# Router scores with the tokens as stationary operand, and five stages moved in a hand-written schedule of two expert layers on one Trainium2 core

## The reference

```python
x = x + L0_xattn(_layernorm(x), ids, ctx, ctx, ctx)      # 4 experts of 256 rows, one per token
x = x + L0_ffn(_layernorm(x), Wg, W1, W2, W3)            # 8 experts of 176 rows, two per token

# layer 2
scores = jnp.einsum('btd,ed->bte', x, Wg)
topk_s, topk_i = jax.lax.top_k(scores, TOP_K)
probs = jax.nn.softmax(topk_s, axis=-1)
...
    h = jax.nn.silu(jnp.einsum('btd,hd->bth', x, W1[e])) * jnp.einsum('btd,hd->bth', x, W2[e])
    y = y + w[..., e:e + 1] * jnp.einsum('bth,dh->btd', h, W3[e])
```

## Time and profile before

| | |
|---|---|
| median of 3 runs | 169.12 us (169.01 to 169.64) |
| the profiled execution, its own time | 168.78 us |
| its span in the trace | 167.0 us |
| PE busy | 153.6 us (92%) |
| DVE busy | 111.9 us (67%) |
| ACT busy | 67.0 us (40%) |
| POOL busy | 59.7 us (36%) |
| HBM | 52 GB/s over the span |

### The profile page before, as it was taken

The page is one execution under the profiler, slowest core; times in us unless marked ns, Lnnn a source line. Parts: engine busy times, 40 slices in busy tenths (PEclk is TensorE's granted clock), DMA queues, the critical chain, the costliest instruction groups (busy, mean ns, idle before and its releaser), DMA issues.

```text
span 167.0 us, 2431 instructions
## 1 busy us (share of the span) xinstructions
PE 153.6 (92%) x892; PEld 131.2 (79%) x892; DVE 111.9 (67%) x223; ACT 67.0 (40%) x119; POOL 59.7 (36%) x49
## 2 busy tenths in 40 slices
PE   7399999959999888999999979999999999999991
PEld 2078788738998666888888868888888888888890
DVE  0858998946695957499999792964444744444453
ACT  3266864624616560835437342206222222222210
POOL 0569967829765871459527300000000000000000
PEclk9969999999999999999999999999999999999999
DMA  3975263030330012051000000000000300000003
GB/s 107 327 271 162 57 214 110 0 94 2 98 96 0 0 12 85 4 144 44 0 0 4 0 0 0 2 4 0 0 0 0 113 16 0 0 0 4 2 0 126
DMA packets 4332, 8.76 MB, mean 52 GB/s; under 512 B 736, under 2 KB 864, under 8 KB 4320
## 3 DMA queue, kind: packets, MB, share of 16 engines
q1 hardware_dynamic: 4176, 8.60, 16.2%
q10 hardware_dynamic: 144, 0.00, 0.0%
HBM read 7.55 MB, written 1.05 MB: 52 GB/s over the span
## 4 chain that ended last, share of the span: by engine, by line
PE 48%; DVE 24%; issue 10%; POOL 6%; ACT 6%; DMA 3%; SPq 1%; ACTq 0%; DVEq 0%; POOLq 0%
PE z L669 27%; PE y L694 19%; DVE act L572 6%; DVE act_lo L537 6%; POOL gated L327 4%; DMA raw<-weights_dram 3%; DVE stats L453 2%; ACT act_hi L377 2%; DVE hT_lo L477 2%; POOL w_lo L281 1%; PE y L612 1%; DVE norm L470 1%; DVE x_sb L483 1%; ACT silu L405 1%; DVE gated L562 1%
## 5 line engine op out<-in xcount | busy, mean ns | idle before, releaser
L669 PE MATMUL z<-hT_hi,w_hi 128*128 128x512 f32 x120 | 47.7, 398 | 0.3 <-ACT hT_hi L351 0.2
L669 PE MATMUL z<-hT_hi,w_lo 128*128 128x512 f32 x120 | 47.2, 393 | 0.0
L537 DVE TENSOR_TENSOR act_lo<-act,act_hi 128x512 fp32r<-128x512 f32 x38 | 33.9, 891 | 16.9 <-ACT act_hi L377 16.7
L694 PE MATMUL y<-w_hi,act_lo 128*128 128x256 f32 x152 | 43.2, 284 | 1.2 <-DVE act_lo L537 1.2
L694 PE MATMUL y<-w_hi,act_hi 128*128 128x256 f32 x152 | 43.0, 283 | 0.0
L694 PE MATMUL y<-w_lo,act_hi 128*128 128x256 f32 x152 | 43.0, 283 | 0.0
L405 ACT ACTIVATE silu<-z 128x512 f32<-128x512 f32 x38 | 22.7, 597 | 46.6 <-PE z L669 46.6
L669 PE MATMUL z<-hT_lo,w_hi 128*128 128x512 f32 x120 | 37.5, 393 | 1.9 <-DVE hT_lo L477 1.8
L281 POOL TENSOR_TENSOR w_lo<-raw,w_hi 128x768 fp32r<-128x768 f32 (+1 forms) x15 | 28.2, 1888 | 15.3 <-ACT w_hi L342 15.3
L694 PEld LDWEIGHTS y<-w_hi,act_lo 128*128 128x128 f32 x152 | 29.0, 191 | 3.3 <-DVE act_lo L537 1.8
L377 ACT CAST act_hi<-act 128x512 fp32r<-128x512 f32 x38 | 23.4, 616 | 20.1 <-DVE act L572 19.1
(11 more groups left out here) (51 smaller groups left out, 79.5 us busy)
## 6 DMA issues: line engine op xcount, KB each, us to landing
raw<-weights_dram SPq DMA_DIRECT2D x11, 384.0 KB, 3.2
raw<-weights_dram SPq DMA_DIRECT2D x8, 256.0 KB, 5.2
x_sb<-x_dram SPq DMA_DIRECT2D x4, 256.0 KB, 4.8
out_dram<-x_sb SPq DMA_DIRECT2D x4, 256.0 KB, 2.5
consts_sb<-consts_dram SPq DMA_DIRECT2D x1, 68.0 KB, 3.8
ids_sb<-token_ids_dram ACTq DMA_DIRECT2D x1, 4.0 KB, 4.0
router_raw<-router_dram SPq DMA_DIRECT2D x1, 8.0 KB, 2.8
```

The lines of the kernel that those rows point to most:

```text
L537: nc.vector.tensor_tensor(act_lo[:, i, :], act[:, i, :], act_hi[:, i, :].bitcast(F32), ALU.subtract)\
L669: return nc.tensor.matmul(bank[:], w[b][:, c, cols], tokens[:, h, k, :], **flags)
L694: last = nc.tensor.matmul(o, a[:, q % BUFFERS, rows], w[b][:, c, wd], start=(first and j == 0), stop=(c == CHUNKS[b] - 1 and j == 2), skip ...
```

## The change

Two kinds of edits. First, the router's scores: `route_scores` makes, for each of the four tiles of 128 tokens, six products that add up in 8 columns of `y[h][0]`, with the tokens (`hT_hi` or `hT_lo`, 128x128) as stationary operand and 8 columns of the router as moving operand. That is 24 products a half in place of 4 of 512 columns. The result has tokens on partitions, so the copy `score_rows`, the four `transpose_scores` and the addition of two parts in `best_two` are gone. All 24 now stand behind the wait for both `hT_lo` tiles. Second, moves: for layer 1 half 1, `normalise` goes from q = 5 to 4 and `tokens_lo` from 7 to 6 on DVE, and `tokens_hi` at q = 7 (and for layer 2 half 0, where it was so before) goes ahead of `round_act` on ACT; for layer 2 half 0, `transpose_gates` goes from q = 16 slot 1 to q = 17 slot 0, and `gates_out` from q = 15 to 16; for layer 2 half 1, `best_two` goes from q = 24 to 23. POOL makes the `_lo` part of weight piece (1, 3) behind the gating of step 15 and not ahead of it.

```diff
-    "normalise": (5, 3, 4),
+    "normalise": (4, 3, 4),
     "transpose_tokens": ((7, 0), (6, 0), (6, 1)),
     "tokens_hi": (7, 5, 6),
-    "tokens_lo": (7, 4, 5),
+    "tokens_lo": (6, 4, 5),
     "scores": (None, (7, 0), (7, 0)),
-    "score_rows": (None, 7, 7),
-    "transpose_scores": (None, (7, 1), (7, 1)),
-    "best_two": (None, 7, 8),
+    "best_two": (None, 7, 7),
     "tanh": (None, 7, 8),
     "softmax": (None, 7, 8),
-    "transpose_gates": ((3, 0), (8, 1), (10, 1)),
-    "gates_out": (2, 7, 9),
+    "transpose_gates": ((3, 0), (9, 0), (10, 1)),
+    "gates_out": (2, 8, 9),
...
+LATE_LO = (1, 3)
...
+                if LATE_LO in SPLIT_AT.get(q - 1, ()):
+                    weight_lo(*LATE_LO)
                 for piece in SPLIT_AT.get(q, ()):
-                    if piece not in VECTOR_LO:
+                    if piece not in VECTOR_LO and piece != LATE_LO:
                         weight_lo(*piece)
...
-                first_tokens = (1, 0) in due("tokens_hi", q)
-                if first_tokens:
-                    tokens_hi(1, 0)
+                first_tokens = [way for way in due("tokens_hi", q) if way != (1, 1)]
+                for way in first_tokens:
+                    tokens_hi(*way)
                 if q >= 1:
                     round_act(q - 1)
...
-                dve.wait_ge(scores_T, h + 1)
-                sc = y[h][1][:, 0:HALF_TILES * 2 * EXPERTS2].rearrange("p (t a e) -> p t a e", a=2, e=EXPERTS2)
-                link(nc.vector.tensor_copy(score_part[:], sc[:, :, 1, :]))
-                link(nc.vector.tensor_tensor(score[:], sc[:, :, 0, :], score_part[:], ALU.add))
+                dve.wait_ge(scored, h + 1)
+                link(nc.vector.tensor_copy(score[:], y[h][0][:, 0:HALF_TILES * EXPERTS2].rearrange(
+                    "p (t e) -> p t e", e=EXPERTS2)))
...
                 pe.wait_ge(hT_lo_done, KD * ln_no(1, h) + 1)
-                for k in range(KD):
-                    nc.tensor.matmul(y[h][0][0:2 * EXPERTS2, :], router_hl[:, k, :, :].rearrange("p a e -> p (a e)"),
-                                     hT_hi[:, h, k, :], start=(k == 0), stop=False, skip_group_check=True)
                 pe.wait_ge(hT_lo_done, KD * ln_no(1, h) + KD)
-                for k in range(KD):
-                    last = nc.tensor.matmul(y[h][0][0:EXPERTS2, :], router_hl[:, k, 0, :], hT_lo[:, h, k, :],
-                                            start=False, stop=(k == KD - 1), skip_group_check=True)
+                for i in range(HALF_TILES):
+                    cols = slice(i * P, (i + 1) * P)
+                    for k in range(KD):
+                        for j, (tokens, part) in enumerate(((hT_hi, 0), (hT_hi, 1), (hT_lo, 0))):
+                            last = nc.tensor.matmul(y[h][0][:, i * EXPERTS2:(i + 1) * EXPERTS2], tokens[:, h, k, cols],
+                                                    router_hl[:, k, part, :], start=(i == 0 and k == 0 and j == 0),
+                                                    stop=(k == KD - 1 and j == 2), skip_group_check=True)
                 last.then_inc(scored, 1)
-
-            def transpose_scores(h):
-
-                pe.wait_ge(score_rows_done, h + 1)
-                for i in range(HALF_TILES):
-                    last = nc.tensor.transpose(y[h][1][:, i * 2 * EXPERTS2:(i + 1) * 2 * EXPERTS2],
-                                               score_rows[:, i * P:(i + 1) * P], ident[0:2 * EXPERTS2, 0:2 * EXPERTS2])
-                last.then_inc(scores_T, 1)
```

More of the change, by code:

```diff
@@ L165, in ffn_moe @@
         minus_half = sb("minus_half", [P, TILES])
-        score_part = sb("score_part", [P, HALF_TILES, EXPERTS2])
         score = sb("score", [P, HALF_TILES, EXPERTS2])
@@ L169, in ffn_moe @@
         top_i = sb("top_i", [P, HALF_TILES, 8], U32)
-        score_rows = sb("score_rows", [2 * EXPERTS2, HALF])
         gap = sb("gap", [P, HALF_TILES])
@@ L192, in ffn_moe @@
         hT_hi_done, hT_lo_done = sem("hT_hi_done"), sem("hT_lo_done")
-        scored, score_rows_done, scores_T = sem("scored"), sem("score_rows_done"), sem("scores_T")
+        scored = sem("scored")
         gap_done, th_done = sem("gap_done"), sem("th_done")
@@ L417, in _ @@
                         tokens_hi(*way)
-                for _, hh in due("score_rows", q):
-                    act_e.wait_ge(scored, hh + 1)
-                    nc.scalar.copy(score_rows[:], y[hh][0][0:2 * EXPERTS2, :]).then_inc(score_rows_done, 1)
                 for _, hh in due("tanh", q):
@@ L718, in stages @@
                     route_scores(hh)
-                for _, hh in due("transpose_scores", q, slot):
-                    transpose_scores(hh)
             pe.wait_ge(warm_in, 1)
```

## The result

The changed kernel takes 171.6 us (170.68 to 171.85, 4 executions) against 169.2 of before: ratio 1.0128, 95% interval 1.0086 to 1.0171. It is slower, where the forecast was 1.4 us faster, and 171.6 lies above the upper end of its range, 169.4. The profiled execution took 171.64 us, span 169.8.

What follows compares the result with a forecast made beforehand. PE, busy 92% of the span, was taken to set the time. Terms of -2.1, -0.2 and +0.9 summed to -1.4 us, giving a forecast of 167.6 us against 169.12 before, range 165.3 to 169.4.

Steps and rivals of the forecast that it cites:

- the clock stays at 1.00 behind both: Expected profile sign: PE's granted clock stays at full speed behind the short score products of both layer 2 halves.
- the rival on the clock: Short score products count as idling and lower PE's clock: 169.3 us for one fall, 171.0 for two; chance 0.05 each.
- The price of 24 products: Layer 2 scores: each short product takes 0.119 us, so 2.85 us a half, bounds 1.7 and 4.6.
- The tokens of half 1: Layer 1 half 1: hT_lo starts earlier, at 32.8, shortening PE's wait in up(8): -2.1 us, bounds -2.4 to -1.3.
- Half 0, scores and gates: Layer 2 half 0: PE's wait for gate_rows goes, up(18) waits about 0.28 us and starts slightly earlier: -0.2 us.
- Half 1: Layer 2 half 1: scores wait 0.4 us for the second hT_lo, then 24 products take 2.85 us: +0.9 us.
- the sentence that I let DVE's lag behind PE stand: Layer 2, 70 to 95 us: DVE's lag behind PE was assumed unchanged, as its work hangs on the same gates.

Runs made afterwards that it cites:

- e2: The kernel before with only the new score form, 24 products of 8 columns a half, all else in its old place: median 172.31 us, ratio 1.021 to before.
- e6: e1 with normalise of layer 1 half 1 back at q = 5: median 165.52 us, ratio 0.979 to before.
- e9: The changed kernel with normalise at 5 and 16 score products a half, their 16 moving columns repeated to 128: median 165.27 us, ratio 0.983 to before.
- e12: e9 with the gates of layer 2 half 0 at their old place: median 164.67 us, ratio 0.984 to before.
- e3: The changed kernel with the router's 8 moving columns repeated to 128 in each score product: median 168.44 us, ratio 1.000 to before.
- e1: The kernel before with the moves alone, scores in their old form: median 167.01 us, ratio 0.990 to before.
- a_again: The changed kernel itself, taken again later: median 171.44 us over 10 executions, ratio 1.006 to before.
- e5: The changed kernel with the router's 8 moving columns repeated to 32 in each score product: median 170.21 us, ratio 0.999 to before.
- e14: The changed kernel with normalise at 5 and the gates at their old place: median 167.63 us, ratio 0.996 to before.
- e13: e6 with 48 extra products of 8 columns in one piece behind down(30) in layer 2, result unused: median 175.39 us.
- e11: e6 with the gates of layer 2 half 0 back at their old place: median 164.58 us, ratio 0.981 to before.

## Why the prediction was wrong

- **The step that failed** is "the clock stays at 1.00 behind both", with the rival on the clock at 0.10. The mechanism stood in that rival with its price (1.7 us a fall; measured 1.66 and 1.69), but I gave it one chance in ten and cut the range below it. The argument against it was that PE's idle 1.81 us in the earlier trace rows had not brought the clock down. That was one execution, and in e2's profile a fall follows the same wait; and the short products last longer than that wait, 2.6 us, which the argument didn't weigh.
- **The rival's own number was right by luck.** It gave 171.0 for two falls, and 171.6 was measured; but its 171.0 rests on a gain of 1.4 that wasn't there. By spans, 167.0 to 169.8, the two falls are +3.35, the three terms below about -0.2, and a further -0.4 lies ahead of `up(7)`, where the start of the program, which the change doesn't touch, went faster in this execution.
- **The price of 24 products**, 2.85 us a half: 2.60 and 2.67 measured. The load sets the pace, 0.108 to 0.111, the 0.11 that the earlier trace rows gave, and not the 0.119 that I preferred. Right to 0.25 us a half. The figure of 25 ns a short product that the Trainium skill gives ("TensorE: Matmul & The Clock Gate", "Back-to-back issue gap") is for products without their loads, as that section says itself; where each product has a load of its own the trace shows 0.108 us.
- **The tokens of half 1**, -2.1: about -1.1 (8.24 to 7.10 us from `up(7)` to `down(5)`). The mechanism was right, and the size lay below my lower bound of 1.3. I let `hT_hi` stay and knew of the delay by `normalise`; that `normalise` takes 1.0 us longer at its new place wasn't in the sum, nor that `router_hl` would hold `hT_lo` back to 33.31. `hT_hi` starts 3.96 us after `up(7)` where it was 3.61. e6 gets 2.4, the whole of it.
- **Half 0, scores and gates**, -0.2: from the scores to `up(18)` 14.78 us against 13.58, of which the fall is 1.66, so -0.5 without it; half 0 came out as worked out, 0.25 of it by the cheaper products. From the first transpose of the gates to `up(18)` it is 2.16 us (69.13 to 71.29), to the hundredth as forecast, with PE standing still 0.29 for 0.28.
- **Half 1**, +0.9: from `up(23)` to `up(24)` 8.14 against 6.53, +1.6, of which `down(20)` gives 0.13 to the clock, and `up(24)` saves the 0.1 that I had counted: about +1.4. The wait for `hT_lo` is 1.1 and not 0.4: the sentence that I let DVE's lag behind PE stand was wrong. `hT_lo` starts 2.5 us after `up(23)` where it was 1.9, since DVE begins layer 2 behind the moved gates (70.46 for 68.31, with `up(17)` a microsecond earlier). The gates' place alone shows it: PE's idle time there is 0.96 us in e9 and 0.37 in e12, which differ in nothing else.
- **The sum without falls.** -1.1 - 0.5 + 1.4 is -0.2, where I had -1.4. At clock 1.00 e3 measures 167.56 against 167.59, nothing. The fastest executions share it out: the moves gain 1.4 (e1, 166.18), and the score form at a full clock costs 1.4 (e3 above e1). So the change had two faults: the moves and the new form cancelled, and the clock took 3 us on top. The first alone would have given 169.2, inside the range.
- **The range** was added up too narrowly by a little: the forecast's lower bound is 167.6 - 0.3 - 0.6 = 166.7 and not 166.9. Nothing hangs on it.

## What to carry to other kernels

Replacing wide products by many of a few columns costs a load each (here 0.108 us for 128 columns), whatever moves, and can cost more behind them: the granted clock fell to 1.2 GHz behind 24 such products in both of its profiles, and 11 of 14 executions are at a mean clock of 0.977 or below. Moving the same columns 16 times over is free in time and, in most executions, keeps the clock up. When a stage is moved on a hand-written schedule, move one at a time: of this change's moves one lost 1.2 us at DVE and one 0.9 by starting the next layer late, out of what the others gained, and each could be seen in one row of the engine that idled. And a wait that leaves the clock alone in one profile may bring it down in the next; look at the spread of executions before arguing from it.

## What the runs showed of the hardware

A moving operand read 16 times over by a repeated access pattern took no longer than one read once, as long as the load was the longer (2.62 against 2.60 us for 24). A fall of the clock behind the scores lasted 3.4 us in seven cases (two each in the changed kernel and a_again, one each in e5, e14 and half 0 of e2), but 6.8 us in half 1 of e2 and 10.2 us in e13, the two where it began while the short products still ran. At the lower level a load of 128 columns sets a pace of about 0.21 us where it is 0.108 at the full clock: the 48 products of e13 show both.

Four DVE copies of 128 columns took 0.63 us alone (e11) and 2.20 beside a subtraction on POOL. The rows look as if one of the two stands still until the other is done: the copies start at 63.47 and end 0.49 us after POOL's piece (63.34 to 65.18). In the profile of before it is the other way about: `act_lo` keeps its 0.68 at 30.04, and POOL's piece beside it takes 2.46 in place of 1.8. DVE's subtraction with an operand in PSUM (`hT_lo`, 1.27 for two) took no longer beside POOL's gating.
